# Four centring additions of a layer norm go from VectorE to GpSimd, and VectorE makes its four row sums first

## The reference, cut to what matters

```python
def _layernorm(x, axis=-1, eps=1e-05):
    m = jnp.mean(x, axis=axis, keepdims=True)
    v = jnp.var(x, axis=axis, keepdims=True)
    return (x - m) / jnp.sqrt(v + eps)
...
    h = jnp.maximum(_layernorm(x, axis=-1), 0.0)
    Wh = h @ W
    e = (Wh @ a1)[:, None] + (Wh @ a2)[None, :]
    e = jax.nn.leaky_relu(e, negative_slope=ALPHA)
    scores = jnp.where(adj > 0, e, jnp.float32(NEG_INF))
    attention = jax.nn.softmax(scores, axis=1)
    x = x + jax.nn.elu(attention @ Wh)
```

## Time and profile before

| | |
|---|---|
| median of 3 runs | 743.15 us (742.93 to 743.79) |
| the profiled execution | 743.62 us |
| its span on the core | 741.7 us |
| outside the span | 1.92 us |
| VectorE, TensorE, ScalarE, GpSimd busy | 694.1, 655.4, 636.4, 55.4 us |

### The profile page before, as it was taken

One profiled execution on the slowest core, in us unless ns is written; L12 is line 12 of the kernel. 1 busy time (PEld: TensorE's weight loads), 2 busy tenths in 40 slices (PEclk: granted clock), 3 DMA queues, 4 the chain that ended last, 5 costly groups with the idle time before them and its releaser, 6 DMA issues.

```text
span 741.7 us, 24886 instructions
## 1 busy us (share of the span) xinstructions
PE 655.4 (88%) x10422; PEld 638.1 (86%) x10422; DVE 694.1 (94%) x769; ACT 636.4 (86%) x361; POOL 55.4 (7%) x47
## 2 busy tenths in 40 slices
PE   5853998989999898989999898989899898989891
PEld 5643998989999898989899898989899898989891
DVE  7797999999999999999999999999999999999961
ACT  5587998989989898989989898989899898989830
POOL 1000000200101010100001010102001010101000
PEclk9975999999999999999999999999999999999996
DMA  9663999999999999999999999999999999999600
GB/s 319 257 261 123 396 421 419 408 420 405 421 399 421 414 406 421 401 421 402 420 398 421 409 412 419 399 422 402 420 398 422 403 416 414 406 421 402 270 17 8
DMA packets 42882, 275.02 MB, mean 371 GB/s; under 512 B 4976, under 2 KB 9072, under 8 KB 10096
## 3 DMA queue, kind: packets, MB, share of 16 engines
q1 hardware_dynamic: 41024, 270.55, 89.9%
q0 software_dynamic: 1536, 4.20, 1.5%
q10 hardware_dynamic: 304, 0.03, 0.0%
HBM read 272.66 MB, written 2.10 MB: 370 GB/s over the span
## 4 chain that ended last, share of the span: by engine, by line
DVE 64%; issue 17%; PE 9%; ACT 4%; DVEq 3%; DMA 1%; POOL 0%; ACTq 0%
DVE code L437 34%; DVE work L451 20%; PE psum L693 4%; PE psum L691 3%; ACT work L335 2%; PE psum L676 1%; DVE code L444 1%; DVE parts L458 1%; DVEq L436 1%; DVE sums L463 1%; DVE fill L470 1%; DVE sums L474 1%; ACT trow L309 1%; PE psum L632 1%; DVE V L537 1%
## 5 line engine op out<-in xcount | busy, mean ns | idle before, releaser
L691 PE MATMUL psum<-V,work 128*128 128x130 f16 x4096 | 505.0, 222 | 6.1 <-DVE work L451 5.8
L693 PE MATMUL psum<-V,work 128*128 128x130 f16 x4096 | 505.2, 224 | 0.0
L335 ACT ACTIVATE work<-trow,ns 128x4096 int8<-128x4096 f32 x128 | 474.7, 3708 | 0.0
L691 PEld LDWEIGHTS psum<-V,work 128*128 128x128 fp8e4 x4096 | 407.7, 100 | 11.7 <-issue 10.5
L693 PEld LDWEIGHTS psum<-V,work 128*128 128x128 fp8e4 x4096 | 404.0, 99 | 0.0
L437 DVE TENSOR_SCALAR code<-adj_ring 128x4096 uint8<-128x4096 int32 x128 | 292.5, 2285 | 0.0
L676 PE MATMUL psum<-identb,code 128*128 128x128 bf16 x2048 | 140.1, 223 | 53.3 <-DVE code L444 45.2
L342 ACT ACTIVATE work<-psum 128x1024 f32<-128x1024 f32 x128 | 131.1, 1024 | 56.8 <-DVE work L451 29.5
L676 PEld LDWEIGHTS psum<-identb,code 128*128 128x128 bf16 x2048 | 122.6, 100 | 59.1 <-DVE code L444 47.6
L451 DVE TENSOR_SCALAR work<-work 128x1024 int32<-128x1024 int32 x256 | 164.8, 686 | 2.7 <-PE psum L693 2.7
L444 DVE SCALAR_TENSOR_TENSOR code<-work,code 128x1024 int32<-128x1024 int32 x128 | 156.6, 1224 | 7.5 <-ACT work L335 4.8
(11 more groups left out here) (78 smaller groups left out, 134.1 us busy)
## 6 DMA issues: line engine op xcount, KB each, us to landing
adj_ring<-in_adj SPq DMA_DIRECT2D x256, 1024.0 KB, 8.3
work<-in_x SPq DMA_DIRECT2D x4, 512.0 KB, 6.1
xg<-in_x POOLq DMA_DIRECT2D x16, 128.0 KB, 7.7
out_y<-res POOLq DMA_DIRECT2D x16, 128.0 KB, 6.4
W<-in_L_gnn_W ACTq DMA_DIRECT2D x2, 16.0 KB, 4.4
a_sb<-in_L_gnn_a ACTq DMA_DIRECT2D x1, 0.5 KB, 4.9
```

The costliest lines, as they stand in the source:

```text
L335: nc.scalar.activation(sign[:, k % 2].bitcast(I8), trow[:, h * UW:(h + 1) * UW], ACT.Sign, bias=ns[:, B:B + 1] if isinstance(B, int) else ...
L691: nc.tensor.matmul(sums_of[:, 0:FP], up8[:, j // 2, j % 2], V[:, jb, 0:FP], start=h == 0 and j == 0, stop=False, skip_group_check=True)
L693: last = nc.tensor.matmul(sums_of[:, FP:2 * FP], down8[:, j // 2, j % 2], V[:, jb, FP:2 * FP], start=False, stop=h == 1 and j == HB - 1, s ...
```

## The change

GpSimd makes the four additions (a new function `centre(b)` behind its two copies of W); each waits for that block's minus mean, and for the addition before it. VectorE makes the row sums and minus means of all four blocks in a row (`means(b)`), and then the rest of its prologue in the order that it had. Nothing else is edited.

```diff
 # GpSimd
+                def centre(b):
+                    pool.wait_ge(s_nm, b + 1)
+                    nc.gpsimd.tensor_tensor(xh[:, out_of(b)], xh[:, out_of(b)],
+                                            stat[:, 1, out_of(b)].unsqueeze(2).to_broadcast([P, RR, F]), ALU.add)\
+                        .then_inc(s_xc, 1)
+
                 pool.wait_ge(s_const, 7)
                 pool.wait_ge(s_w, 48)
                 nc.gpsimd.tensor_copy(Wx[0:F, 0:F], W2[0:F, :]).then_inc(s_Wcopy, 1)
                 nc.gpsimd.tensor_copy(Wx[F:P, FX:FX + F], W2[F:P, :]).then_inc(s_Wcopy, 1)
+                pool.wait_ge(s_Wcopy, 2)
+                for b in range(NR):
+                    if b:
+                        pool.wait_ge(s_xc, b)
+                    centre(b)
...
 # VectorE
-                def centre(b):
+                def means(b):
...
                     nc.vector.tensor_scalar(stat[:, 1, r], stat[:, 0, r], -1.0 / F, None, ALU.mult).then_inc(s_nm, 1)
-                    dve.wait_ge(s_nm, b + 1)
-                    nc.vector.tensor_tensor(xh[:, r], xh[:, r], stat[:, 1, r].unsqueeze(2).to_broadcast([P, RR, F]),
-                                            ALU.add).then_inc(s_xc, 1)
...
-                centre(0)
-                centre(1)
+                for b in range(NR):
+                    means(b)
                 variance(0)
-                centre(2)
                 variance(1)
                 copy_Wh(0)
-                centre(3)
                 variance(2)
                 copy_Wh(1)
                 variance(3)
```

## The result

The changed kernel takes 738.68 us (median of 7, 737.29 to 739.49) against 743.15 of the kernel before (median of 7, 740.62 to 743.79). The ratio is 0.9945, 95% interval 0.9929 to 0.9962: faster by 0.4 to 0.7%. In two later sets of runs the ratio was 0.9958 (0.9943 to 0.9972) and 0.9950 (0.9933 to 0.9967), 3.2 and 4.4 us between the medians. I had forecast 743.2 with a range from 741.1, so the changed kernel is some 4 us faster where I saw nothing.

A forecast was written before the change was run, and what follows sets the result against it. VectorE's own instruction chain bounds the body, and the prologue's last `Wh` copy sets its start. 4.9 us of removed additions were offset by held minus means: net +0.06 us, so 743.2 us against 743.15, range 741.1 to 746.0.

The forecast's parts named there:

- The body: VectorE's instruction chain from 66.01 us: unchanged in length, its end moving only as its start does.
- The price of one addition: GpSimd's addition over 1024 columns in the prologue: 2.35 us each, with 1.6 and 4.6 kept for the range.
- The copy's slope: GpSimd's rate taken from a 64-column copy: 2.2 ns a column above a fixed 0.10 us.
- my own sum: Whole kernel: span 741.7 + 0.06, plus 1.92 outside, 743.7 for a profiled execution; 743.2 for the median.
- The hold: Prologue: VectorE's minus mean waits for GpSimd's running addition, so the two alternate with a pitch of 2.35 + 0.2 us.
- first rival: Prologue: minus means slip past GpSimd's additions unheld, last copy of `Wh` at 26.7, 1.1 us below, 742.0; chance 0.22.
- The walk: Step-by-step timing of the changed prologue across four engines: last copy of `Wh` ends at 27.85 us, +0.06.
- The old order's walk: Same step-by-step timing of the prologue before the change: ends at 27.8 us against 27.72 measured.
- and so: TensorE in the prologue: busy from 12.9 to 24.0 but for half a microsecond, hence clocked at 2.4 GHz.
- The load of `xg`: First load on GpSimd's queue moves from 7.89 to some 18 us and costs nothing.
- moved as one: Steps behind the last copy of `Wh` up to the body shift together, its end carried one to one to the time.
- VectorE's busy time is 4.9 us smaller: Sign to look for: VectorE's busy time falls 4.9 us, its idle time ahead of 28 us grows as much.

The follow-up runs named there:

- padded kernels: The kernel before with 1, 4 (twice) or 8 idle one-column memsets in VectorE's wait ahead of the body; 738.67 to 739.42 us.
- e4: Changed kernel plus four one-column memsets on VectorE in its wait ahead of the body, putting back the four instructions; 740.44 us, ratio 0.9972 to the kernel before.
- e5: Kernel before plus four one-column memsets on VectorE in its wait ahead of the body; 738.67 us, ratio 0.9967.
- e13: Kernel before plus four one-column memsets in VectorE's wait ahead of the body, run a second time; 739.42 us, ratio 0.9975.
- e16: Kernel before plus one memset in VectorE's wait ahead of the body; 738.93 us, ratio 0.9966.
- e17: Kernel before plus eight memsets in VectorE's wait ahead of the body; 739.01 us, ratio 0.9961.
- e7: Changed kernel plus four scratch operations in GpSimd's wait for the weights (memset and copy of 1024 columns, additions of 512 and 64) to measure prices; copy 1.04 us.
- e3: Changed kernel with the four minus means made by GpSimd too, so none of VectorE's meets an addition; 739.33 us, ratio 0.9956 to the kernel before.
- e10: Changed kernel with the four minus means made by ScalarE; 737.99 us, ratio 0.9949 to the kernel before.
- e1: Kernel before with the order alone: all four sums and minus means first, additions still on VectorE; 744.74 us, ratio 1.0032.
- e6: Changed kernel with a 512-column memset on GpSimd ahead of each addition, behind its wait; 738.76 us, ratio 0.9955 to the kernel before.

## Why the prediction was wrong

Two terms failed: the body, which I put at nothing, and the price of an addition. They are taken in turn, with the steps that held.

**The body "neither shortens nor lengthens with this change, which touches nothing in it".** This is the step that failed most. The pass of the loop became 0.12 us shorter, 1.7 us in all, 40% of the gain in the two profiles, and by the medians of the padded kernels more than half. I had taken "the same instructions" for "the same time". e4 takes it away from the changed kernel, and e5, e13, e16 and e17 give it to the kernel before. Why the distance matters stays open.

**The price of one addition, 2.35 us.** It was 1.90. The copy's slope was wrong: I divided the 0.14 us that 64 columns take above a memset of one column, and most of that 0.14 was fixed cost of a copy (e7: 0.19 us fixed, 0.83 ns a column). With 1.90 and a first addition that starts 0.3 us earlier, my own sum would have given 3 x 0.45 + 0.3, so some 1.6 us less: about what the profiles show for the prologue (1.4 to 1.7, below). The figure of the Trainium skill (GPSIMD Engine Reference, section 3.1), halved to an estimate of 2.25 us, fits the estimate from the additions of e7, 2.3 us, but not the kernel's own additions, and my 2.35 came near it by luck.

**The hold.** As a mechanism it was right in each detail: the second minus mean took until 9.5, the end of the addition, the third and fourth until the ends of theirs, so the hold works in the direction that the trace of before did not show. The Trainium skill (SBUF — State Buffer, "Who interferes with whom") has both directions, and the trace agrees: 1.62 and 0.92 us for an instruction of 0.17. As a price it was wrong. My first rival, "no hold", promised 1.1 us; e3 and e10, without the hold, gain 0.2 to 0.3, since ScalarE then comes last.

**The walk.** It had variance(0) at 15.5 (13.61), Wh 3 from 24.9 (22.6), and the end of the last copy at 27.85 (25.42). Of the 2.4 us at the end 1.9 stand already at variance(0): 3 x 0.45 are the additions, 0.3 the start of the first (7.60 instead of 7.9), and 0.2 rounding. The other 0.5 lies behind it, where VectorE took 11.8 us to the end of the last copy and not 12.35. The old order's walk, 27.8, met the 27.72 of a trace that has 0.6 us of fallen clock in it, against 27.10 to 27.16 without; so some of that agreement was luck. A walk of 40 steps through four engines that hits a known trace to 0.1 us does not have that precision for another order.

**What lies under the measured 2.3 us.** 0.6 of it is TensorE's clock, which fell in the kernel before's profile and not in three of its four padded versions (27.10 to 27.16). The change itself is worth the rest: 1.4 to 1.7 us between those and the 25.42 to 25.69 of the changed kernel's prologue. That the walk has TensorE busy through 20 to 22 us, and its clock at 2.4 GHz behind that, came out:

```profile
20.00:22.00 2.00, 1.97 (x18) 1.77 (x16) 1.93 (x6) 1.53 (x3) 0.00 (x0) 1.00 1.01 397
22.00:24.00 2.00, 1.36 (x12) 1.39 (x13) 1.38 (x4) 0.00 (x0) 0.00 (x0) 1.00 1.02 426
```

(windows of the changed kernel's first profile, against the earlier trace rows). The "and so" between the two is not shown: in e5, e13 and e16 TensorE stood idle for half of 20 to 22 just as in the kernel before, and its clock stayed at 1.00. So this gain belongs to an execution, and not surely to the change.

**The rest.** The load of `xg` at 15.7 instead of 7.9 cost nothing, and everything from 25.4 to 63.7 moved as one, as written, in every version but e1. The slices of the earlier trace rows were misread: the third is 9, and the fourth, with the wait ahead of the body in it, is 7; nothing rests on it. "VectorE's busy time is 4.9 us smaller" was wrong by the held 2.9 us: it fell by 1.9. The sum in the two profiles: prologue 2.28, body 1.65, end 0.29, together 4.2 us, the difference of the spans.

## What to carry to other kernels

Before you promise that a loop costs the same, compare the start of each pass in both traces; an instruction more or less ahead of it can be worth as much as the change under study, and trying one idle instruction in a wait is cheap. Price an operation from a row of its own size: a slope from a row of 64 columns is mostly fixed cost. And an instruction that is held up counts as busy and looks like a bound; only a run without the hold tells whether something else would have come last anyway, as it did here but for 0.2 to 0.3 us. When a run is to test a term, look in its trace whether the term was there: in e6 it was not.

## What the runs showed of the hardware that was not expected

- One place in VectorE's loop waits 0.29 or 0.16 us in every pass but the first (there 0.54 or 0.17), by how many instructions stand in the program ahead of the loop (41.43 or 41.30 us a pass); no other value was seen at six distances. The cause is open.
- TensorE's granted clock fell in some executions and not in others with the same work ahead of it: TensorE was busy for 0.97 of the 2 us from 20 to 22 in five profiles of the old prologue, and the clock in the next 2 us was 0.50 in two of them and 1.00 in three.
- A GpSimd addition of 1024 float32 columns with a second input that repeats 16 numbers takes 1.90 us, while plain additions of 512 and 64 columns take 1.26 and 0.32, which makes an estimate of 2.3 for 1024.
- GpSimd's memset also holds a minus mean of VectorE: in e6 the one that starts at 7.92, beside the memset of 7.82 to 8.34, takes 0.45 us instead of 0.17.
